# Layer 1's keys and values in its decay stage, z scaled by two engines, and products over all eight PSUM banks

## The reference

```python
    x = x + _L0_attn_ref(_layernorm(x, axis=-1), L0_attn_Wq, L0_attn_Wk, L0_attn_Wv)
    ...
    x = x + _L1_attn_ref(_layernorm(x, axis=-1), L1_attn_decay_logit, L1_attn_W, L1_attn_b, L1_attn_conv_w, L1_attn_conv_b)
    x = x + _L1_xattn_ref(_layernorm(x, axis=-1), ctx_1024, ctx_1024, L1_xattn_Wq, L1_xattn_Wk, L1_xattn_Wv, L1_xattn_Wo, L1_xattn_bo)
    ...
    x = x + _L3_attn_ref(_layernorm(x, axis=-1), L3_attn_W_attn, L3_attn_b_attn, L3_attn_W_proj, L3_attn_b_proj, L3_attn_rel_pos_emb)
```

## Time and profile before

| | |
|---|---|
| median of 3 runs | 2992.48 us (2991.68 to 2994.76) |
| the profiled execution | 2990.36 us, span 2989.1 us |
| TensorE, busy | 2530.3 us, 85% of the span |
| weight loads of TensorE | 1743.6 us, 58%, beside its products |
| VectorE | 1251.4 us, 42% |
| ScalarE | 817.7 us, 27% |
| POOL | 521.5 us, 17% |
| granted clock of TensorE, mean | 0.907 |
| DMA | 189.48 MB, mean 63 GB/s |
| chain of waits that ended last | TensorE 78%, VectorE 14%, ScalarE 2% |

### The profile page before, as it was taken

One profiled execution on the slowest core, in us unless ns is written; L12 is line 12 of the kernel. 1 busy time (PEld: TensorE's weight loads), 2 busy tenths in 40 slices (PEclk: granted clock), 3 DMA queues, 4 the chain that ended last, 5 costly groups with the idle time before them and its releaser, 6 DMA issues.

```text
span 2989.1 us, 34376 instructions
## 1 busy us (share of the span) xinstructions
PE 2530.3 (85%) x13778; PEld 1743.6 (58%) x13798; DVE 1251.4 (42%) x2347; ACT 817.7 (27%) x2275; POOL 521.5 (17%) x454
## 2 busy tenths in 40 slices
PE   4776999974799597887899999699956999876999
PEld 4664777763477363422466666587832688733555
DVE  7553111128288764556333322300044355656220
ACT  0110111112276161354222221122203344304220
POOL 1521222211200101211244310222220100002000
PEclk8977999996899798999899999699975999987999
DMA  4003443420100000300000000323227423100000
GB/s 147 0 29 137 165 164 143 175 83 20 45 2 15 34 1 1 117 0 26 3 1 1 0 1 1 121 82 93 72 87 295 168 87 128 36 25 1 8 8 14
DMA packets 73749, 189.48 MB, mean 63 GB/s; under 512 B 9551, under 2 KB 52949, under 8 KB 65654
## 3 DMA queue, kind: packets, MB, share of 16 engines
q1 hardware_dynamic: 65590, 169.11, 15.8%
q0 software_dynamic: 8000, 18.18, 1.9%
HBM read 143.88 MB, written 46.09 MB: 64 GB/s over the span
## 4 chain that ended last, share of the span: by engine, by line
PE 78%; DVE 14%; ACT 2%; issue 2%; POOL 1%; DMA 1%; SPq 0%; POOLq 0%; DVEq 0%; ACTq 0%
PE psum L219 42%; PE psum L3054 6%; PE psum L1248 4%; PE psum L1579 4%; PE psum L1595 4%; PE psum L1584 3%; PE psum L2100 2%; PE psum L1610 2%; PE psum L2087 2%; PE psum L3063 2%; PE psum L2774 2%; DVE stats L251 2%; DVE z L265 1%; PE psum L1575 1%; PE psum L379 1%
## 5 line engine op out<-in xcount | busy, mean ns | idle before, releaser
L219 PE MATMUL psum<-arena 128*128 128x256 f32 (+7 forms) x4172 | 1009.3, 401 | 33.7 <-DVE arena L3150 13.2
L219 PEld LDWEIGHTS psum<-arena 128*128 128x128 f32 (+4 forms) x4176 | 732.2, 182 | 300.5 <-issue 148.8
L1669 DVE TENSOR_REDUCE small<-psum 128x4 f32<-128x1024 f32 (+1 forms) x112 | 136.9, 1223 | 151.7 <-PE psum L1584 108.7
L261 POOL TENSOR_SCALAR x_moments<-x_moments 128x4 f32<-128x4 f32 x48 | 12.2, 253 | 1036.2 <-DVE x_moments L254 1036.1
L1291 DVE TENSOR_TENSOR arena<-arena,psum 128x256 f32<-128x256 f32 x138 | 57.9, 420 | 318.4 <-ACT arena L1263 318.4
L1141 POOL DMA_INDIRECT l_out<-arena,slot_tables x86 | 85.6, 995 | 494.3 <-ACT arena L1269 288.5
L3054 PE MATMUL psum<-arena 128*128 128x512 bf16 x752 | 165.4, 379 | 0.8
L1644 ACT ACTIVATE arena<-psum,small 128x128 f32<-128x128 f32 (+1 forms) x384 | 149.0, 416 | 44.4 <-DVE small L1669 44.4
L1680 DVE COPY arena<-psum 128x512 f32<-128x512 f32 x224 | 143.3, 680 | 1.6 <-PE psum L1595 1.5
L379 PE MATMUL psum<-ident,z 128*128 128x128 f32 x256 | 47.2, 345 | 111.6 <-DVE z L265 83.8
L1248 PE MATMUL psum<-arena 128*128 128x256 f32 x552 | 136.5, 392 | 0.0
(11 more groups left out here) (327 smaller groups left out, 3567.1 us busy)
## 6 DMA issues: line engine op xcount, KB each, us to landing
arena<-L_ffn_w_in SPq DMA_DIRECT2D x23, 2176.0 KB, 9.2
arena<-L_ffn_W_in SPq DMA_DIRECT2D x16, 1024.0 KB, 8.2
positions<-arena SPq DMA_DIRECT2D x16, 1024.0 KB, 3.9
arena<-positions SPq DMA_DIRECT2D x16, 1024.0 KB, 8.0
arena<-l_out SPq DMA_DIRECT2D x16, 512.0 KB, 8.1
positions<-arena SPq DMA_DIRECT2D x16, 512.0 KB, 3.4
arena<-positions SPq DMA_DIRECT2D x16, 512.0 KB, 9.0
l_out<-arena SPq DMA_DIRECT2D x2, 2048.0 KB, 13.8
```

Source lines behind the costliest of these rows:

```text
L219: last = nc.tensor.matmul(out, lhsT, rhs, start=(n == 0), stop=(n == len(pairs) - 1))
L1669: nc.vector.reduce_max(self.minus_top(h), use.bank(u).rearrange("p (h l) -> p h l", l=L), AX_X, negate=True).then_inc(self.topped.up(), 1)
```

## The change

It has three parts.

1. `Uses` deals out eight banks in every stage, 6 and 7 among them, where the transposes of `z` go as well; the transposes and the products wait for each other's copies through the same table as before. Areas of L3Attention get banks 0 to 3 and 4 to 7 in turn.
2. Of each group's four tiles of `z`, VectorE writes two. ScalarE writes the other two as `x * rstd + shift` (`act_z`). POOL computes the shift, mean times rstd, negated, in two small instructions behind the root (`pool_shift`). Who waits for `z` now waits for two engines.
3. A new class, `L1Context`, holds what L1Attention does with the context: the nine loads, the keys, the values. SP issues the loads at the start of L1Decay. In TensorE's queue the keys of a group stand behind the transposes of the same group, and the values of two tiles stand ahead of each `out`. ScalarE alone copies these keys and values out; POOL clears the values' array at the start of L1Decay. L1Attention is left with queries, attention and the last product. The slabs are laid out anew for it.

The diff, cut to its core:

```diff
-    def __init__(self, k, first=0, count=6):
+    def __init__(self, k, first=0, count=8):
...
+    def pool_shift(self, g, out, shifted):
+
+        k, nc, at = self.k, self.k.nc, slice(4 * g, 4 * g + 4)
+        k.pool.wait_ge(self.rooted, g + 1)
+        k.pool.step(nc.gpsimd.tensor_tensor(out[:, at], self.out[:, at, 0], self.out[:, at, 2], ALU.mult))
+        nc.gpsimd.tensor_scalar(out[:, at], out[:, at], -1.0, None, ALU.mult).then_inc(shifted.up(), 1)
+
...
-        self.z = k.counter("z_written", "dve").reserve(TILES)
+        self.z = [k.counter("z_written_by_" + e, e).reserve(TILES // 2) for e in ("dve", "act")]
+        self.shifted = k.counter("x_shift", "pool").reserve(GROUPS)
...
         for g in self.next("z", last):
             self.k.dve.wait_ge(self.moments.rooted, g + 1)
-            for i in range(4 * g, 4 * g + 4):
-                self.moments.scaled(self.k.z, i).then_inc(self.z.up(), 1)
+            for i in (4 * g, 4 * g + 1):
+                self.moments.scaled(self.k.z, i).then_inc(self.z[0].up(), 1)
+
+    def act_z(self, last):
+        k = self.k
+        for g in self.next("z_act", last):
+            k.act.wait_ge(self.shifted, g + 1)
+            for i in (4 * g + 2, 4 * g + 3):
+                k.nc.scalar.activation(k.z[:, i, :], k.x[:, i, :], ACT.Identity, scale=k.x_moments[:, i, 2:3],
+                                       bias=k.x_shift[:, i:i + 1]).then_inc(self.z[1].up(), 1)

     def dve_zT(self, last):
         self.dve_z(last)
...
         self.moments.pool(g)
+        self.moments.pool_shift(g, k.x_shift, self.shifted)
...
     def act_final(self, g):
+        self.act_z(g - 1)
         self.act_twice(g - 1)
...
+class L1Context:
+    def __init__(self, k, uses):
+        self.k, self.uses, s, d = k, uses, k.slab, k.d
+        self.ctxT = k.arena[:, 26624:30720].rearrange("p (c t) -> p c t", c=DC)
+        self.kT = s[4].rearrange("p (c t) -> p c t", c=DC)
+        self.values = k.arena[:, 5 * SLAB:5 * SLAB + 6144]
+        self.wq, self.wk, self.wv = (weight(s[8], 512 * n, DC, D) for n in range(3))
+        self.wo, self.bo = weight(s[8], 2000, DC, D), s[8][:, 2512:2768]
+        self.fetch = Fetch(k, *[(self.ctxT[:, c, :], d[f"ctxT_{c}"]) for c in range(DC)],
+                           *[(w, by_chunk(d["L1_xattn_" + n])) for w, n in
+                             ((self.wk, "Wk"), (self.wv, "Wv"), (self.wq, "Wq"), (self.wo, "WoT"))],
+                           (self.bo, d["L1_xattn_bo"].to_broadcast([P, D])), signal="context_loaded")
+        self.keys = Features(k, uses, self.kT, self.wk, self.ctxT, 0)
+        self.v = self.values.rearrange("p (x n e) -> p x n e", n=3, e=HD)
+        self.pairs = PairValues(k, uses, self.v, self.wv, self.ctxT, 0)
+        self.cleared = k.counter("values_cleared", "pool").reserve(1)
+    def done(self):
+        return self.keys.done(GROUPS - 1) + self.pairs.done()
+    def pool(self):
+        self.k.nc.gpsimd.memset(self.values, 0.0).then_inc(self.cleared.up(), 1)
 class L1Decay(Stage):


-        self.out = [u.add("dve") for _ in range(TILES // 2)]
+        self.context, self.out = L1Context(k, u), []
+        k.context = self.context
+        for g in range(GROUPS):
+            self.context.keys.add(("act", "act"))
+        for n in range(TILES // 2):
+            self.context.pairs.add("act")
+            self.out.append(u.add("dve"))
...
         pe.wait_ge(self.fetch.loaded)
-        self.norm.pe_zT(GROUPS - 1)
+        for g in range(GROUPS):
+            self.norm.pe_zT(g)
+            self.context.keys.pe(g, [(self.context.fetch.loaded,)])
         for n, u in enumerate(self.out):
+            self.context.pairs.pe_pair(n)
             pe.wait_ge(self.state_in, n // 2 + 1)
             pe.wait_ge(self.conv_in, n // 2 + 1)
...
                                      scale=self.keep[:, c:c + 1]).then_inc(self.fed_in.up(), 1)
+            if g:
+                self.context.keys.act(g - 1)
...
-        for g in range(GROUPS):
-            self.next.norm.act_final(g)
+        self.context.keys.act(GROUPS - 1)
+        for n in range(TILES // 2):
+            self.context.pairs.empty_pair(n, "act", (self.context.cleared, 1))
+            if n % 2:
+                self.next.norm.act_final(n // 2)
...
     def pool(self):
+        self.context.pool()
     def sp(self):
-        self.k.sp.wait_ge(self.conv_in)
-        self.k.sp.wait_ge(*self.uses.filled(self.out[-1]))
-        self.next.fetch.sp()
+        self.context.fetch.sp()
...
+    def pe_pair(self, n):
+        k, u = self.k, self.use[n]
+        bank = self.uses.take(u)
+        for j in range(2):
+            i = 2 * n + j
+            pairs = [(self.src[:, c, P * i:P * i + P], self.w[:, c, :]) for c in range(DC)]
+            mm = products(k.nc, bank[:, D * j:D * j + D], pairs)
+        mm.then_inc(self.uses.fills(u), 1)
...
+        self.k, s = k, k.slab
+        self.q = [s[n].rearrange("p (c t) -> p c t", c=DC) for n in (0, 1)]
+        context = self.context = k.context
+        self.fetch = context.fetch
         self.norm = Norm(k)
-        self.bias = Bias(k, self.norm, self.bo)
+        self.bias = Bias(k, self.norm, context.bo)
         u = self.uses = Uses(k)
-        self.keys = Features(k, u, self.kT, self.wk, self.ctxT)
-        self.queries = Queries(k, u, self.q, self.wq, k.zT)
-        v = self.values.rearrange("p (x n e) -> p x n e", n=3, e=HD)
-        self.pairs = PairValues(k, u, v, self.wv, self.ctxT, TILES)
-        scores, turned = ([s[n][:, 1024 * m:1024 * m + 1024] for m in range(4)] for n in (6, 7))
-        self.attention = Attention(k, u, CAUSAL_WORK, self.q, self.kT, v, self.ctxT, scores, turned)
-        self.product = Product(k, u, None, self.ctxT, self.wo, self.bias)
+        self.queries = Queries(k, u, self.q, context.wq, k.zT)
+        scores, turned = ([s[n][:, 1024 * m:1024 * m + 1024] for m in range(4)] for n in (2, 3))
+        self.attention = Attention(k, u, CAUSAL_WORK, self.q, context.kT, context.v, k.zT, scores, turned)
+        self.product = Product(k, u, None, k.zT, context.wo, self.bias)
         u.close()
-        self.cleared = k.counter("values_cleared", "pool").reserve(1)
-        self.before = self.keys.done(3) + self.queries.done(3) + self.pairs.done()
+        self.before = context.done() + self.queries.done(GROUPS - 1)

     def pe(self):
         self.k.pe.wait_ge(self.fetch.loaded)
         for g in range(GROUPS):
-            self.keys.pe(g, [])
-        for g in range(GROUPS):
             self.norm.pe_zT(g)
             self.queries.pe(g, self.norm.zT_in(g))
-        self.pairs.pe(lambda i: [])
         self.attention.pe(self.before)
         self.product.norm = self.next.norm
         self.product.pe(lambda i: [self.attention.done(i // 4 * 4 + 3)])

-    def projected(self, engine):
-        head = self.norm.dve_zT if engine == "dve" else self.norm.act_zT
-        for g in range(GROUPS):
-            self.keys.empty(g, engine)
-        for g in range(GROUPS):
-            head(g)
-            self.queries.empty(g, engine)
-        self.pairs.empty(engine, (self.cleared, 1))
-
     def act(self):
-        self.projected("act")
+        for g in range(GROUPS):
+            self.norm.act_zT(g)
+            self.queries.empty(g, "act")
         self.attention.act(self.before)
         self.product.act()

     def dve(self):
-        self.projected("dve")
+        for g in range(GROUPS):
+            self.norm.dve_zT(g)
+            self.queries.empty(g, "dve")
         self.attention.dve(self.before)
         self.product.dve()

```

95 lines of the change are left out of this document (51 added, 44 removed).

## The result

The changed kernel takes 2956.11 us (median of 4 runs, 2954.02 to 2958.15), the kernel before 2993.62 beside it (4 runs): a ratio of 0.9875, 95% interval 0.9858 to 0.9892, so 37.4 us less. The forecast was 2947, 45 less; the measured time lies in its range, near rival B's and C's 2957 and 2956. The profiled execution took 2954.02 us (span 2952.7), 36.4 less span than before.

A forecast was written before the change was run, and what follows sets the result against it. TensorE bounds on average (85% of the span), with holes where it waits for context load, taps and PSUM copies. Context -22.9, areas -21.0, z and banks -1.3 sum to -45.2: 2990.36 to 2945.2, on the median's scale 2947; range 2935 to 2963.

The forecast's parts named there:

- rival B: L3Attention's areas: stores run at only 340 GB/s, 10.4 us more, so 2957; chance 0.15.
- Rival C: Decay stage of layer 1: TensorE's clock stays at 0.50, the context part gives only 14, so 2956; chance 0.15.
- the first four rows of the table: Forecast to L0Mixture's last statistics -3.0, layer 1's first score -22.9, L3Attention's first area +4.95, first query behind the areas -21.0.
- Rival D: L3Attention's areas: banks bring no gain, stores already the limit or areas not alternating, so 2968; chance 0.03.
- Term 1: Layer 1: context, keys and values in the decay stage bring attention's start from 811.15 to 788.3, -22.9 us.
- They are there at 703.3: L1Decay: context loads, issued some 692.6, let the keys start 10.7 us later, at 703.3.
- An `out` of two tiles costs 2 x 1.31: L1Decay: each `out` of two tiles takes TensorE 2.62 us, eight cost 21.0, with no more waiting.
- 18.8 again, plus 3.1: L1Attention: queries take 18.8 us as before, plus 3.1 for an uncovered last evacuation and ScalarE's z(3) behind another.
- Terms 3 and 4: Stage ends: z by two engines -4.5, banks 6 and 7 +3.2 at L1Attention to MoD; net -1.3, bounds -8 and +8.
- the second of its two readings: VectorE's z beside POOL's memset at 986.57: one tile carries the whole memset, so halving the tiles saves 0.67, not 1.9.
- At the program's start -1.2, -1.8 into L0Mixture: First stage ends: z by two engines saves 1.2 us at the program's start and 1.8 into L0Mixture.
- The last stretch: From the first query behind L3Attention's areas to the program's end: forecast -3.25 us.

The follow-up runs named there:

- areas_alone: Kernel before, with only the 32 areas of L3Attention taking banks 0 to 3 and 4 to 7 in turn: 2972.52 us, ratio 0.9938.
- context_alone: Changed kernel with six banks (eight in L2Cosine) and all of z by VectorE, leaving the context part alone: 2975.01 us, ratio 0.9948.
- keys_late: Changed kernel, in L1Decay keys of groups 1 to 3 behind group 3's transposes, ScalarE's key copies behind the middle tap: 2941.63 us, ratio 0.9832.
- keys_late_areas: keys_late joined with eight_in_areas, ScalarE copying keys 0 after half of the middle tap: 2937.89 us, ratio 0.9817.
- six_banks: Changed kernel with products dealt over six banks again, eight only in L2Cosine: 2961.58 us, ratio 0.9902.
- eight_in_areas: six_banks, but L3Attention's 32 areas take banks 0 to 3 and 4 to 7 in turn: 2946.32 us, ratio 0.9851.
- z_by_dve: Changed kernel with its eight banks, all of z written by VectorE again and no shift on POOL: 2960.99 us, ratio 0.9892.
- first_bank: Changed kernel with only L0Autocorrelation's deal of banks beginning at bank 1 instead of 0: 2945.39 us, ratio 0.9852.
- memset_later: keys_late with POOL's memset of the values moved behind the taps of group 0: 2944.46 us, ratio 0.9842.
- z_early: keys_late_areas with ScalarE's z of group 3 heading its queue in L1Attention, L1MixtureOfDepths and L3Attention: 2926.67 us, ratio 0.9790.
- best_order: z_early with eight banks dealt out in L1Decay too: 2921.10 us, ratio 0.9772.

## Why the prediction was right, and where it was off

**Right: direction, range, and two of three mechanisms.** In the trace the stretches fell 12.65 us short of the forecast in the first four rows of the table and gave 3.95 back in the last, which is spread; so the total is nearer to the forecast than its terms. The areas were sized by the DMA row and came out at that: batch 7.84 us for 7.8, phase 20.5 us shorter for 21.0, and the wait moved to the stores. By the ratios the areas gave 18.6 us alone and 15.3 beside the rest. Rival B, the slower stream, is refuted: 416 GB/s in the middle of areas_alone, 414 between 2250 and 2290 here. Rival D, no gain, falls with it. The sentence of the Trainium skill (DMA: Bandwidth & Descriptors, "Where 436 GB/s comes from") that some 358 GB/s bind between HBM and SBUF does not hold for one core by these runs; the row did.

**Term 1, mis-sized: -22.9 against -16.4 in the trace, -15.6 alone.** The mechanism held (taps late by the keys ahead of the transposes, landing 11.2 us after issue). Three numbers in its working were off, and they add up to the 6.5 us. "They are there at 703.3": "some 692.6" for SP's first issue was read 0.7 too early, since the stage's first instruction on VectorE stood at 693.34, 1.90 behind the last statistics, and SP's first issue comes just as far behind them in context_alone; POOL's shift, which SP waits for, adds 0.3 (2.20 in the change); and the load took 11.24 us (694.97 to 706.21), not 10.7. The first `out` comes 0.9 later for all this. "An `out` of two tiles costs 2 x 1.31": the first two cost double, since TensorE had been idle for 4.52 us ahead of them, 2.6. "18.8 again, plus 3.1": ScalarE's z of group 3 made the last transposes wait 2.42 us, and behind them the queries took 6.08 us instead of 3.67, 3.0. The wait alone doesn't explain the low clock: keys_late and keys_late_areas have it and take 6.00 and 5.75 us, but in six_banks and eight_in_areas the same 2.42 us (779.88 above) are followed by queries of 3.67 at a granted clock of 1.00. What decides between the two is open. Rival C named the low clock, but as one that stays through the stage; here it came in short stretches, each behind a wait. The hole at 726 to 730 stood in the prediction as what speaks for C, and should have been in the sum.

**Terms 3 and 4: -1.3 was -6.5 by the runs and +0.4 by the table's three stretches, out of larger numbers of both signs.** z by two engines, -4.5 in the sum, is worth 5.1 us in the kernel with eight banks (z_by_dve), and 13.7 between context_alone and six_banks, of which 3.8 are the clock in the areas. The prediction counted gains at five stage ends and losses at two; the traces of context_alone and six_banks part by 1 to 4 us in most stages, in L2Attention, where +1.2 was forecast, by -3.1, and in L2Cosine, where +1.25 was, by +0.5. The working priced z by one group that nothing delays. The 0.67 us that it takes for z beside POOL's memset stands in none of its terms; there the change has 3.08 us for two tiles (977.67), where four took 3.79: 0.71, as the second of its two readings had it. That VectorE's queue carries two groups' z at a stage's end, so that each halved one moves all that stands behind it, is my reading of why; no run tries it by itself.

Against it stand the banks. The prediction looked for harm at banks 6 and 7, where transposes stand, and found it, but too small: +3.2 was 5.0, the wait of 3.18 us at 967.38 and 1.8 more for the products behind it, at a granted clock of 0.67 (1.00 in six_banks). The stretch was +6.3 for 4.95. It did not ask where the deal ends in one stage and begins in the next: the step "At the program's start -1.2, -1.8 into L0Mixture" needed the first product of L0Autocorrelation to have a free bank. It started at 68.51 for 60.98 in six_banks; first_bank shows this cause by itself. The stretch was +1.3 for -3.0.

**The last stretch** (-7.2 for -3.25) is spread as far as it exceeds the forecast: in first_bank and keys_late, with the same instructions there, L3Convolution and the last stage together took 4.8 us longer than in the changed kernel's profiled execution.

The parts measured one after the other give context -15.6, z -13.7, areas -15.3, eight banks elsewhere +7.2. They add up to -37.4, the result, because each is the difference to the run before it. That the sum comes out says nothing for the single parts: in another order z is worth 5.1 and the areas 18.6.

## What to carry to other kernels

Filling a hole with independent work is worth the whole hole only if the filler stands behind everything that the critical chain still needs from that engine's in-order queue; here one order of the same instructions was worth 12.9 us more than another. Where a resource is dealt out in turn, follow the deal across stage borders: the first user after a reset meets the last one before it. A hole of a few us ahead of dense work on TensorE can also cost what comes behind it, at half clock: 2.6 us behind a hole of 4.52, 1.8 behind one of 3.18, 2.4 behind a wait of 2.42 in three kernels and nothing behind the same wait in two. In a sum it belongs in the bounds at least.

## What the runs showed of the hardware

- A memset of 5.22 us on POOL held up a VectorE TENSOR_SCALAR of 128x2 elements from 0.17 to 3.70 us, until about the memset's end; but the same memset beside VectorE's taps (SCALAR_TENSOR_TENSOR, both inputs in SBUF) cost them nothing: 22.66 us for 32 with it and without it (memset_later and the earlier trace rows). Two tiles of z took 3.08 us beside a memset of 2.66 (the change, 977.67), four tiles 3.79 before. The prediction had spoken of the lock as if it held against any VectorE instruction. The Trainium skill (SBUF — State Buffer, "Who interferes with whom") is narrower: `tensor_scalar` in its fast mode contends with GpSimd, and an instruction with two SBUF inputs only with a GpSimd instruction that reads SBUF. The memset's row names no source; the 3.70 us and the unchanged 22.66 us agree with it.
- Stores from SBUF to DRAM ran at 416 GB/s with the DMA engines' share at 1.02 over 40 us (areas_alone, 2260 to 2300).
- Two executions of the same instructions in L1Attention and the stage after parted by 8 us (z_early and best_order), with more time at half clock in the longer one (granted 0.95 for 0.97 through attention).
- A wait of TensorE of 2.42 us was followed by half clock in three kernels (queries of 6.08, 6.00 and 5.75 us) and by full clock in two (3.67 us in six_banks and eight_in_areas), with the same instructions in that stage.
